# Attention with P computed transposed, run as one program with the routing of a decoder layer (one core)

## The reference

```python
x = x + mixer(layernorm(x))            # projections, conv, a scan over time, gates
x = x + xattn(layernorm(x), ctx, ctx)
x = x + moe(layernorm(x))

# xattn: 16 heads of 16, causal
q, k, v = Q @ WQ + bQ, K @ WK + bK, V @ WV + bV
scores = where(causal, q @ k.T * SCALE, -inf)
out = softmax(scores) @ v
return out @ WO + bO

# moe: top 2 of 8 experts, capacity int(1.25 * N * 2 / 8) + 1 = 641 rows per expert
probs = softmax(x @ router_w.T); k_probs, k_idx = top_k(probs, 2)
# each (token, expert) pair takes the next free row of its expert, in token order; pairs over capacity are dropped
h = silu(buf @ w1); out_buf = h @ w2
return sum(pair_out * k_probs) + x
```

## Time and profile before

| | |
|---|---|
| Median of 3 runs | 873.04 us (870.11 to 873.97) |
| The profiled execution | 866.73 us |
| Its span, first to last instruction | 864.9 us |
| PE busy, matmul | 684.1 us, 79% |
| PE busy, weight load | 597.3 us |
| DVE busy | 599.8 us, 69% |
| ACT busy | 434.1 us, 50% |
| POOL busy | 349.4 us, 40% |

### The profile page before, as it was taken

One profiled execution on the slowest core, in us unless ns is written; L12 is line 12 of the kernel. 1 busy time (PEld: TensorE's weight loads), 2 busy tenths in 40 slices (PEclk: granted clock), 3 DMA queues, 4 the chain that ended last, 5 costly groups with the idle time before them and its releaser, 6 DMA issues. The chain is left out here.

```text
span 864.9 us, 15113 instructions
## 1 busy us (share of the span) xinstructions
PE 684.1 (79%) x4776; PEld 597.3 (69%) x4792; DVE 599.8 (69%) x1285; ACT 434.1 (50%) x971; POOL 349.4 (40%) x322
## 2 busy tenths in 40 slices
PE   3759979889752199888988666509999999999992
PEld 2538768777542066666666556508999999999992
DVE  6685786867841089999999686704877877877831
ACT  4555736535411077777777311104655655655641
POOL 1357352343403000000000437752477777777755
PEclk9898999999975599999999765557999999999997
DMA  9102018230211611111111423223055255251213
GB/s 299 29 26 88 24 50 291 71 117 20 88 49 49 204 37 49 47 45 44 49 48 26 140 80 104 78 67 132 5 143 148 30 145 147 30 146 18 27 22 41
DMA packets 54857, 70.35 MB, mean 81 GB/s; under 512 B 10843, under 2 KB 45542, under 8 KB 54800
## 3 DMA queue, kind: packets, MB, share of 16 engines
q1 hardware_dynamic: 45584, 61.82, 22.1%
q0 software_dynamic: 9216, 7.81, 6.3%
HBM read 42.57 MB, written 28.79 MB: 83 GB/s over the span
## 5 line engine op out<-in xcount | busy, mean ns | idle before, releaser
L1114 ACT ACTIVATE a_pr<-a_scores,a_nm 128x128 f32<-128x128 f32 (+1 forms) x256 | 90.6, 426 | 80.8 <-DVE a_nm L1186 77.6
L1694 DVE SCALAR_TENSOR_TENSOR w_v<-w_th,w_bank 128x324 f32<-128x324 f32 x128 | 62.9, 492 | 70.6 <-ACT w_th L1424 69.3
L1563 PE MATMUL w_bank<-w_w2h,w_hh 128*108 128x256 f32 x384 | 108.6, 283 | 0.5 <-POOL w_hl L1349 0.5
L1563 PE MATMUL w_bank<-w_w2h,w_hl 128*108 128x256 f32 x384 | 107.8, 281 | 0.0
L1563 PE MATMUL w_bank<-w_w2l,w_hh 128*108 128x256 f32 x384 | 107.5, 280 | 0.0
L1424 ACT ACTIVATE w_th<-w_bank 128x324 f32<-128x324 f32 x128 | 56.6, 442 | 100.0 <-PE w_bank L102 99.9
L1349 POOL TENSOR_TENSOR w_hl<-w_v,w_hh 128x324 fp32r<-128x324 f32 x64 | 56.4, 882 | 91.5 <-ACT w_hh L1430 91.5
L1183 DVE TENSOR_REDUCE a_mx<-a_scores 128x2 f32<-128x512 f32 (+1 forms) x96 | 65.4, 681 | 34.1 <-remote 33.5
L1365 POOL IOTA w_x<- 128x16 uint32 x1 | 0.2, 191 | 205.9 <-POOLq L1077 205.9
L102 PE MATMUL w_bank<-w_xh,w_w1h 128*128 128x324 f32 x256 | 81.1, 317 | 1.1 <-ACT w_xh L1419 1.1
L102 PE MATMUL w_bank<-w_xh,w_w1l 128*128 128x324 f32 x256 | 80.8, 316 | 0.0
(11 more groups left out here) (230 smaller groups left out, 1995.6 us busy)
## 6 DMA issues: line engine op xcount, KB each, us to landing
w_s<-in_L_ffn_w SPq DMA_DIRECT2D x16, 1024.0 KB, 5.9
disp<-c_blank SPq DMA_DIRECT2D x8, 658.1 KB
w_rows<-disp SPq DMA_DIRECT2D x8, 658.1 KB
vd<-m_vs SPq DMA_DIRECT2D x4, 816.0 KB, 3.7
a_vs<-vd SPq DMA_DIRECT2D x1, 3264.0 KB, 11.1
g_x<-in_x SPq DMA_DIRECT2D x4, 512.0 KB, 7.9
m_cin<-in_ctx SPq DMA_DIRECT2D x4, 512.0 KB, 4.3
kd<-m_qkh SPq DMA_DIRECT2D x4, 512.0 KB, 2.9
```

What stands on the lines that cost most here:

```text
L1114: ins = act.activation(pr[:, u % 2, j * n:(j + 1) * n], sbank[u % 3][:, j * n:(j + 1) * n], ACT.Exp, bias=nm[:, u, j:j + 1], scale=SCALE)
L1563: mm = pe.matmul(eb[t // 2][0:SP_, (t % 2) * D:(t % 2 + 1) * D], a[:, g % 3, s], w2_piece(b, f), start=f == 0 and t % 2 == 0 and n == 0, s ...
L1694: dve.scalar_tensor_tensor(v[:, n % 4, :], th[:, n % 2, :], 1.0, hb[n % 3][:, 0:HALF], ALU.add, ALU.mult).then_inc(F["v"], 1)
```

## The change

Attention and the third block become one block, `attention_route_experts`. The numbers of PE matmuls, DMAs and the order of all engines in it are new; the mixer changes only where V and WO are made ready, and the experts' loop is as it was.

- Work goes in 16 items g (batch b, half k of the heads), three units each, 48 steps t in all; each unit is now 1024 columns. The non-transposed scores (`scores`, L1363) run 6 steps ahead and serve for the row maxima alone. The three products of a split are stacked on the contraction rows instead (16 rows each for high x high, high x low, low x high: `q3`, `k3`, 48 rows, two heads in the two halves of the partitions), so a head takes one matmul.
- The maxima are transposed (`turn_maxima`), split in two (`maxima_high` on ACT, `maxima_low` on DVE, tile `a_mt`) and copied by SP into two more rows of `q3`, against rows of -1 in `k3`: 16 DMAs per item (`maxima`, L1091). `lay` takes 12 DMAs per item (L1082).
- `turned` makes the scores again with keys on partitions, maxima subtracted (50 rows, L1389); ACT takes the exponential of 1024 columns at once into `pr` in fp32. No P is transposed, split or scaled.
- `weigh` (L1411) has V (16 columns of a head in a strip of 32) and a matrix of ones as fp32 stationary operands of 32 columns, `pr` as fp32 moving operand, and four heads' outputs in four strips of 32 PSUM partitions. The output comes out transposed; `divide` multiplies by a reciprocal of 256 columns, and `project` takes it as it is, in fp32, with WO's rows laid in that order by 8 DMAs.
- The routing of block i runs beside attention from step 12 i + 14 on (`due`, with the offsets PROJECT, BOTH, NORM, TURN, LOGITS, RANKS, SEND), the first expert's weight splits too.
- V is written to DRAM in fp32 in strips of 32 columns (`value`); `v_first`, `v_second`, `v_rest`, `v_third` and the split of WO go.

```diff
-def attention(nc, sems, c, qd, kd, vd, o_sb):
...
-def output_route_experts(nc, sems, c, x_sb, o_sb, woh, wol, bo, router_w, disp, w1, w2, out):
+def attention_route_experts(nc, sems, c, x_sb, bo, wo_w, router_w, qd, kd, vd, disp, w1, w2, out):
...
+    PROJECT, BOTH, NORM, TURN, LOGITS, RANKS, SEND = 8, 14, 16, 17, 20, 23, 24
...
+                for g in range(GR):
+                    if ITEMS <= g + 2 < GR:
+                        lay(g + 2)
+                    maxima(g)
...
+                def scores(u):
...
+                        mm = pe.matmul(sbank[:, at:at + keys], q[rows, p, tok], kx[rows, p, 0:keys], start=False,
+                                       stop=True, skip_group_check=True)
...
+                        mm = pe.matmul(tbank[:, at:at + w], kx[rows, p, key], q[rows, p, tok], start=False, stop=True,
+                                       skip_group_check=True)
...
+                for t in range(-LEAD, END):
+                    u = t + LEAD
+                    if batch_due(t) is not None:
+                        project(batch_due(t))
...
+                    if 0 <= t < NS:
+                        turned_mask(t)
+                    if 0 <= t < NS:
+                        turned(t)
+                    if t % 3 == 0 and 0 <= t // 3 + 1 < GR:
+                        turn_maxima(t // 3 + 1)
+                    if 1 <= t <= NS:
+                        weigh(t - 1)
+                    if u < NS:
+                        mask(u)
+                        scores(u)
...
+                def maxima(u):
...
+                    dve.tensor_reduce(dst, src, AX.X, ALU.max).then_inc(A["nm"], 1)
...
+                for t in range(-LEAD, END):
+                    u = t + LEAD
+                    if u < NS:
+                        maxima(u)
+                    if t % 3 == 0 and 0 <= t // 3 + 1 < GR:
+                        maxima_low(t // 3 + 1)
+                    if t % 3 == 0 and 1 <= t // 3 <= GR:
+                        divide(t // 3 - 1)
+                    if batch_due(t) is not None:
+                        x2(batch_due(t))
```

More of the change, by code:

```diff
@@ L314, in _ @@
                 sp.wait_ge(S["k_st"], 32 * NBLK)
-                for n in range(2):
-                    sp.wait_ge(S[f"v_st{n}"], 16 * NBLK // 2)
+                sp.wait_ge(S["v_st"], 16 * NBLK)
                 sp.wait_ge(S["blanked"], 16 * E)
@@ L382, in _ @@
                     if i == 0:
[L383 to L388, removed]
+                        pool.memset(vf[:, :, :], 0.0).then_inc(S["vzero"], 1)
                     if last and now:
@@ new lines, in mask @@
+                def mask(u):
+                    s = u % 3
+                    ge(pe, A["nm"], u)
+                    for e in range(2):
+                        bank = sbank[:, e * 4 * P:(e + 1) * 4 * P]
+                        out = bank.rearrange("q (p k) -> q p k", p=4) if s == 0 else \
+                            bank.rearrange("q (p k) -> q p k", p=2)[:, :, P:2 * P]
+                        n = 4 if s == 0 else 2
+                        pe.matmul(out, c["identb"][:, :], c["mask"][:, :].unsqueeze(1).to_broadcast([P, n, P]),
+                                  start=True, stop=False, skip_group_check=True)
@@ new lines, in turned_mask @@
+                def turned_mask(n):
+                    s = n % 3
+                    ge(pe, A["exp"], n)
+                    for e in range(2):
+                        bank = tbank[:, e * 4 * P:(e + 1) * 4 * P]
+                        out = bank.rearrange("k (p q) -> k p q", p=4) if s == 2 else \
+                            bank.rearrange("k (p q) -> k p q", p=2)[:, :, 0:P]
+                        m = 4 if s == 2 else 2
+                        pe.matmul(out, c["mask"][:, :], c["identb"][:, :].unsqueeze(1).to_broadcast([P, m, P]),
+                                  start=True, stop=False, skip_group_check=True)
@@ new lines, in turned @@
+                def turned(n):
+                    g, s = divmod(n, 3)
+                    if s == 0:
+                        pe.wait_ge(A[f"m_in{g % 2}"], 256 * (g // 2 + 1))
+                    q, kx = q3[g % ITEMS], k3[g % ITEMS]
+                    for p, e in heads(g, s):
+                        rows = slice(64 * e, 64 * e + 3 * HD + 2)
+                        tok = slice(P, L) if s == 2 else slice(0, L)
+                        key = slice(P, L) if s == 2 else slice(0, P)
+                        w = P if s == 2 else L
+                        at = e * 4 * P + (p if s == 2 else p % 2) * w
+                        mm = pe.matmul(tbank[:, at:at + w], kx[rows, p, key], q[rows, p, tok], start=False, stop=True,
+                                       skip_group_check=True)
+                    mm.then_inc(A["st"], 1)
@@ new lines, in project @@
+                def project(b):
+                    if b == 0:
+                        pe.wait_ge(S["rw"], 16 * 9)
+                    pe.wait_ge(A["o"], 2 * b + 2)
+                    if b % 2 == 0:
+                        ge(pe, S["xt"], b)
+                    else:
+                        pe.wait_ge(S["x2"], b)
+                    for t in range(2):
+                        for k in range(DC):
+                            at = (b % 2) * L + t * P
+                            mm = pe.matmul(bank0[:, t * D:(t + 1) * D], ot[:, k, at:at + P], wo[:, k, :],
+                                           start=k == 0, stop=k == DC - 1)
+                    mm.then_inc(S["y"], 1)
```

627 lines of the change are left out of this document (278 added, 349 removed).

## The result

The changed kernel takes **918.86 us** (median of 4 runs, 916.89 to 920.03) against 871.58 of the kernel before in runs beside it: ratio 1.0546, 95% interval 1.0497 to 1.0595. Slower, as forecast, but by 47 us instead of 19; the time lies inside the range of 850 to 930. The profiled execution took 918.31 us with a span of 916.6.

A forecast was written before the change was run, and what follows sets the result against it. Bound: a per-item loop through SP's DMAs of the maxima, 16.0 us against 11.7 before. Start, fifteen periods, last units and tail put the experts 18.8 us later: 885.5 profiled, plus 6.3 to the median, 892 us; range 850 to 930.

The forecast's parts named there:

- Start of item 0: Start of the first item's turned scores, after SP's 61 load issues and the first maxima: forecast at 317.1 us.
- Fifteen periods: Fifteen item-to-item intervals in the attention loop, at 16.0 us each, ending at 557.1 us.
- Last three units: End of attention: three units' turned scores, exponential and handover, and the last P times V: 7.5 us, to 564.6.
- Tail: From the last P times V to the experts: reciprocal, projection, residual, statistics, routing; 41.5 us, experts starting at 606.1.
- the term of SP: SP's 16 one-row DMAs of maxima per item: 0.46 us each, last issued 6.9 us after the first.
- the chain: Per-item loop from turned scores through new scores, maxima and SP's DMAs to the next turned scores: 16.0 us.
- SP's own load: SP's queue per item: 16 maxima issues, 12 of `lay` and half a load of V, 13.1 us.
- the rival in line: P times V does not run side by side: 3.6 instead of 1.7, 17.9 us per item, 920 us; chance 0.14.
- P times V side by side at 1.7: On TensorE, 16 fp32 matmuls of P times V in four column groups cost 1.7 us per item.
- The clock rival: TensorE stays at 2.4 GHz and P times V is cheap: period 13.9 us, 860 us; chance 0.19.
- Cheap issue: SP issues one-row DMAs in 0.25 us, engines bound at some 11 us per item: 817 us; chance 0.04.
- The likeliest case's own range: Span of the main forecast: 14.9 to 17.5 us per item, 876 to 915 us; chance 0.55.

## Why the prediction was right in direction and wrong in size

The experts started 33.0 us later than forecast (639.15 against 606.1), and the terms of my sum split it:

- **Start of item 0**, forecast 317.1, measured 319.08: +2.0. SP began earlier, but its 61 issues took 30.1 instead of 28.1, and the burst 10.1 instead of 7.4.
- **Fifteen periods**, 16.0 forecast, 17.72 measured: +25.8. This is the error.
- **Last three units**, 7.5 forecast, 9.2 measured (584.84 to 594.0): +1.7.
- **Tail**, 41.5 forecast, 45.15 measured: +3.65. The projection has eight records in the trace, two for each of its four fp32 matmuls, and takes 3.78, not 2.2, and the last P times V reaches VectorE's reciprocal only 1.55 us after it ends.

The step that failed is the term of SP: "0.46 each with the gap. The last of 16 is issued 15 x 0.46 = 6.9 after the first". I took it from the earlier trace rows, loads of 16 rows from DRAM, and used it for copies of one row within SBUF. These take 0.62, the last is issued 9.4 after the first, and the burst holds SP for 10.0. That puts 2.5 on the chain.

The second half of the error is in the same paragraph: "SP's own load ... is 13.1 us". It is 17.3: 10.0 for the burst, 6.8 for `lay` instead of 5.5, because about one issue per item takes 1.2 to 1.8 us, and 0.5 for the rest. I had called `lay` hidden under 7.1 us of other work; it needs nearly all of it, and in five of fifteen items more than there was. That a queue and a chain of 17.3 and 17.6 make 18.0, I had no term for.

The rest of the chain was 0.9 shorter than forecast (6.2 for 7.1 in the item shown). Turned scores, turned maxima and P times V, forecast 3.25 together, took 3.38 (443.31 to 446.69), the mask 0.53 for 0.6, the scores and their end 0.71 for 1.6 (447.22 to 447.93), VectorE 1.54 for 1.64. The scores are the difference: TensorE runs them at the higher level again, 3.9 us after work began.

One reading was wrong though it did little harm. An fp32 matmul has two records in these traces, a transpose one: the logits of the earlier trace rows are `x16` for eight matmuls in the code, the transposes `x8` for eight. So 0.22 us is half of such a matmul. Two that turn the maxima cost 0.95 (319.81 to 320.76), not 0.5, and the four of the projection 3.78, not 2.2. And P times V in line would have been 16 x 0.43 = 6.9 us instead of 3.6, so the rival in line had the wrong price. *P times V side by side at 1.7* stood up: item 15's, at the lower clock and with no maxima to turn, starts 0.43 apart by four matmuls, four times, 1.7 in all (from 585.57). The rival in line, 920, was hit by the time and not by its reason.

At the higher clock the eight matmuls of 256 columns (16 records) take 1.0, from 448.57 to the mask at 449.58. By the Trainium skill's four passes ("FP8 and Floating Point Precision", TensorE Precision Notes), eight in four groups would be 0.85 by an estimate at 2.4 GHz: the trace is within 0.2 of it. The drain on a change of tiling mode, which the Trainium skill states ("TensorEngine Tiling (Array Packing)", Key Properties), does not show ahead of P times V: turned scores begin at 448.14, spaced 0.11 by four, and P times V follows at 448.57, on the beat. Behind it, the 0.16 beyond the estimate may hold one; no run takes it apart.

*VectorE*: 1.22 and 0.42 forecast, 1.23 and 0.40 measured. *Clock*: low after the wait, 0.83 over the stage, inside the 0.6 to 0.9 given. *The clock rival* falls by its condition, and could not have given 13.9 us per item beside an SP load of 17.3. *Cheap issue* falls by its premise, 0.62 instead of 0.25. Its conclusion was half sound: with the burst at 2.4 us the engines bound, but an item costs 14.2 us, and 12.0 only after four more edits. *The reason for the wait* was as forecast, a DMA into `a_q`.

That the time lies in the stated range is luck: the range reached up to the in-line rival, which had another reason and a wrong price. The likeliest case's own range, 876 to 915, did not hold, since it gave the issue no spread: I had kept no dear end for it, although no row showed a copy within SBUF. The direction was no luck. It rested on the loop through SP being longer than the attention of before, and it was.

## What to carry to other kernels

Count the DMAs of a loop and price each on the queue that issues it, before its bytes: here 1 KB and 4 KB cost the same 0.6 us. Where rows can be joined into one DMA, or half of them issued elsewhere, that is the cheapest gain there is. And add up each queue's whole load per turn of the loop beside the chain: where two limits have the same length, an edit that lifts only one of them gains little.

## What the runs showed of the hardware

- A copy within SBUF into one row holds SP's queue 0.60 to 0.63 us, whether it carries 1, 2 or 4 KB, where 64 KB loads of 16 rows by 4 mostly start 0.47 us apart. Eight such copies from ScalarE's queue take 5.0 to 6.4 us, from SP's 4.8 to 5.6.
- About one issue per item on SP's queue takes 1.2 to 1.8 us (13 from 340 to 540 us in the changed kernel), most often a load of `lay`. This, and not a dearer price of each load, makes `lay` 6.8 us instead of 5.6. What it is stays open; no run here takes it apart.
- VectorE's reciprocal costs by column: 1.74 to 1.76 us for 128 x 256, where 128 x 8 took 0.203 and 128 x 4 0.178. That slope gives 1.75; the forecast's 1.6 was added up wrongly from it.
